# Attention's output projection in float16 planes: one more weight product is scaled into range, and the undoing factor moves into the reciprocal row sums

## What is computed

```python
def _mxfp4_matmul(x, codes, scales, block_size=BLOCK):
    w = codes * jnp.repeat(scales, block_size, axis=0)
    return x @ w
...
q = _mxfp4_matmul(x, wq_codes, wq_scales) + bq
k = _mxfp4_matmul(x, wk_codes, wk_scales) + bk
v = _mxfp4_matmul(x, wv_codes, wv_scales) + bv
...
scores = jnp.einsum('bqhd,bkhd->bhqk', q, k) / jnp.sqrt(jnp.float32(HEAD_DIM))
attn = jax.nn.softmax(scores, axis=-1)
out = jnp.einsum('bhqk,bkhd->bqhd', attn, v).reshape(B, S, NUM_HEADS * HEAD_DIM)
return _mxfp4_matmul(out, wo_codes, wo_scales) + bo
```

## Time and profile before

| | |
|---|---|
| median of 3 runs | 992.88 us (992.58 to 993.28) |
| span of the profiled execution | 991.7 us |
| busy: PE / PEld | 927.3 us (94%) / 585.8 us (59%) |
| busy: DVE / ACT / POOL | 718.4 (72%) / 648.1 (65%) / 641.0 us (65%) |
| chain that ended last | PE 75%, DVE 11%, POOL 4%, issue 4%, DMA 3%, ACT 3% |
| `b_out` matmuls | 3 x 256 from L109 to L111, means 367, 281 and 279 ns |
| `b_v` matmuls, 256 columns, float16 | 3 x 256, mean 273 ns each |

### The profile page before, as it was taken

How to read it: one execution, slowest core, us unless ns; L and a number is a source line. 1 busy time by engine, 2 the same in 40 slices (tenths; PEclk the granted TensorE clock), 3 DMA queues, 4 the chain that set the end, 5 groups by cost and what they waited for, 6 DMA issues and landing times.

```text
span 991.7 us, 18415 instructions
## 1 busy us (share of the span) xinstructions
PE 927.3 (94%) x5772; PEld 585.8 (59%) x5772; DVE 718.4 (72%) x2006; ACT 648.1 (65%) x1410; POOL 641.0 (65%) x599
## 2 busy tenths in 40 slices
PE   4999779999999999999999999999999999988967
PEld 3766456556556556555655655655565557775556
DVE  7863389887777777777778777777876689782327
ACT  5634337787777777776876777777776878433511
POOL 2467759896587668779766676776675655246711
PEclk9999989999999999999999999999999999998979
DMA  9968654687676779868886775677565656545782
GB/s 341 394 204 303 234 191 112 129 160 149 97 150 106 154 145 199 187 140 190 169 168 96 135 154 97 138 143 119 100 124 85 119 103 106 174 151 195 282 349 87
DMA packets 302976, 165.57 MB, mean 167 GB/s; under 512 B 278176, under 2 KB 285600, under 8 KB 300832
## 3 DMA queue, kind: packets, MB, share of 16 engines
q1 hardware_dynamic: 297696, 146.56, 63.8%
q0 software_dynamic: 3072, 9.44, 2.8%
q10 hardware_dynamic: 2112, 8.39, 2.1%
HBM read 68.93 MB, written 28.31 MB: 98 GB/s over the span
## 4 chain that ended last, share of the span: by engine, by line
PE 75%; DVE 11%; POOL 4%; issue 4%; DMA 3%; ACT 3%; DVEq 0%; POOLq 0%; ACTq 0%; SPq 0%
PE b_o L109 5%; PE b_o L110 5%; PE b_o L111 5%; PE b_p L109 5%; PE b_p L111 5%; PE b_p L110 5%; PE b_s L109 5%; PE b_s L110 5%; PE b_s L111 5%; PE b_out L109 3%; PE b_out L110 3%; PE b_out L111 3%; PE b_v L109 3%; PE b_v L111 3%; PE b_v L110 3%
## 5 line engine op out<-in xcount | busy, mean ns | idle before, releaser
L2423 POOL TENSOR_TENSOR h<-pr,h 128x512 f16<-128x512 f32 x256 | 293.7, 1160 | 185.9 <-ACT h L1151 180.3
L1141 ACT ACTIVATE pr<-b_s,nmax,kappa 128x512 f32<-128x512 f32 x256 | 197.7, 775 | 39.0 <-DVE nmax L1880 37.6
L1877 DVE TENSOR_SCALAR_CACHE_REDUCE junk<-b_s 128x512 bf16<-128x512 f32 x256 | 175.2, 684 | 30.6 <-PE b_s L111 29.7
L1151 ACT ACTIVATE h<-pr 128x512 f16<-128x512 f32 x256 | 153.7, 627 | 0.5
L1904 DVE SCALAR_TENSOR_TENSOR x<-b_out,rinv,x 128x256 f32<-128x256 f32 x256 | 110.4, 472 | 45.8 <-PE b_out L111 45.8
L109 PE MATMUL b_p<-xh,w 128*128 128x512 f16 x256 | 98.6, 385 | 2.4 <-DVE xh L1681 2.4
L109 PE MATMUL b_s<-kT,qT 128*128 128x512 f16 x256 | 97.6, 381 | 1.0 <-DVE qT L1823 0.7
L110 PE MATMUL b_p<-xh,w 128*128 128x512 f16 x256 | 98.0, 383 | 0.0
L111 PE MATMUL b_p<-xh,w 128*128 128x512 f16 x256 | 98.0, 383 | 0.0
L109 PE MATMUL b_o<-pT,v 128*128 128x512 f16 x256 | 97.1, 379 | 0.0
L110 PE MATMUL b_o<-pT,v 128*128 128x512 f16 x256 | 97.0, 379 | 0.0
(11 more groups left out here) (212 smaller groups left out, 2276.8 us busy)
## 6 DMA issues: line engine op xcount, KB each, us to landing
raw<-in_experts SPq DMA_DIRECT2D x32, 768.0 KB, 7.4
raw_cs<-in_heads SPq DMA_DIRECT2D x16, 1024.0 KB, 5.6
zrows<-zero ACTq DMA_DIRECT2D x4, 2048.0 KB, 17.5
z<-zrows SPq DMA_DIRECT2D x16, 512.0 KB, 4.0
zrows<-zero SPq DMA_DIRECT2D x16, 512.0 KB, 3.1
zl<-zrows SPq DMA_DIRECT2D x16, 512.0 KB, 10.5
rows<-xn SPq DMA_DIRECT2D x8, 512.0 KB, 10.4
pT<-h SPq DMA_TRANSPOSE x256, 3.3
```

Source lines behind the costliest of these rows:

```text
L1141: act.activation(pr[n % 4][:], b_s[n % 3][:], ACT.Exp, bias=nmax[:, u % 2, i:i + 1], scale=kappa[:, s:s + 1], accum_out=rsum[:, u % 2, i:i ...
L1151: act.activation(h[n % 4][:, 0, :], pr[n % 4][:], ACT.Copy).then_inc(q["p_high"], 1)
L1877: dve.tensor_scalar(junk[n % 2][:], b_s[n % 3][:], 0.0, None, ALU.add, ALU.max, accum_out=peaks[:, n % 2:n % 2 + 1]).then_inc(q["peak_read ...
L2423: pool.tensor_tensor(h[n % 4][:, 1, :], pr[n % 4][:], h[n % 4][:, 0, :], ALU.subtract).then_inc(q["p_split"], 1)
```

## The change

`wo` and `oT` become float16 planes. So that both lie in float16's range, the output weights get a power-of-two factor of their own, as v has. `norms`, `bound`, `halves` and the factors get a second column: `vo_scale` and `vo_undo`. `squares` gets a third square, of the product of the output weights, and now waits for all four products (`w_mul` at 4p + 4) and for `qk_normed`, since it writes into `square_qk`; `squares_qk` waits for `normed`. `scales` works on two columns and computes `o_undo`, the product of both undoing factors and a constant; `oT` is made with a fixed factor 2**-23. In `sums` the reciprocal goes into `rsum_o`, and a TENSOR_SCALAR multiplies it by `o_undo` into `rinv`. The output weights are scaled into range on GpSimd (a fourth `range_weights`), are split behind v's in place of ahead of them, and in `prepare` move from r = 5 to r = 7; `load_qk` moves from r = 6 to behind the transposes of r = 7. In the written-out part of pair 1 the products of v and o stand one behind the other.

```diff
 ZBITS = 23
+OBITS = 23
...
 ones = m.keep("ones", [P, P])
-norms = m.keep("norms", [P, 2])
-bound = m.keep("bound", [P, 1])
-halves = m.keep("halves", [P, 1], I32)
+norms, bound = m.keep("norms", [P, 4]), m.keep("bound", [P, 2])
+halves = m.keep("halves", [P, 2], I32)
...
 peaks = m.keep("peaks", [P, 2])
-v_scale = m.keep("v_scale", [P, 2], I32)
-v_undo = m.keep("v_undo", [P, 2], I32)
+vo_scale, vo_undo = (m.keep(n, [P, 2, 2], I32) for n in ("vo_scale", "vo_undo"))
+o_undo, rsum_o = m.keep("o_undo", [P, 2]), m.keep("rsum_o", [P, 4])
...
 w = [[m.at((A, Bm)[s] + 8192 * k, f"w{k}_{s}", [P, 6, D], F16) for k in range(2)] for s in range(2)]
-wo = [[m.at((A, Bm)[s] + 8192 * k + 3072, f"wo{k}_{s}", [P, 2, D], F32R) for k in range(2)] for s in range(2)]
+wo = [[m.at((A, Bm)[s] + 8192 * k + 3072, f"wo{k}_{s}", [P, 2, D], F16) for k in range(2)] for s in range(2)]
...
 zl = [m.at(o, f"zl{i}", [P, 4 * D]) for i, o in enumerate(z_place)]
-oT = [[m.at(Bm + 16384 + 4096 * s + 2048 * k, f"oT{k}_{s}", [P, S], F32R) for k in range(2)] for s in range(2)]
+oT = [[m.at(Bm + 16384 + 4096 * s + 2048 * k, f"oT{k}_{s}", [P, S], F16) for k in range(2)] for s in range(2)]
...
             pe.wait_ge(q["v_sum"], 2 * B * (p - 1) + 7)
-        pe.matmul((b_v[:, 0:2] if p else b_p0[:, D:D + 2]), ones[:], norms[:], start=True, stop=True).then_inc(q["normed"], 1)
+        pe.matmul((b_v[:, 0:4] if p else b_p0[:, D:D + 4]), ones[:], norms[:], start=True, stop=True).then_inc(q["normed"], 1)
...
         if n % (2 * B) == 0:
-            pe.wait_ge(q["aw_ready"], 4 * pair_of(n) + 4)
+            pe.wait_ge(q["aw_ready"], 4 * pair_of(n) + 3)
...
             if u % (2 * B) == 0:
-                pe.wait_ge(q["aw_ready"], 4 * pair_of(u) + 3)
+                pe.wait_ge(q["aw_ready"], 4 * pair_of(u) + 4)
...
     def outputs(u):
-        p = pair_of(u) % 2
...
             act.wait_ge(q["out_done"], 2 * (u - 1))
-        act.activation(oT[u % 2][0][:], b_o[:], ACT.Copy, scale=v_undo[:, p:p + 1].bitcast(F32)).then_inc(q["o_hi"], 1)
+        act.activation(oT[u % 2][0][:], b_o[:], ACT.Copy, scale=2.0 ** -OBITS).then_inc(q["o_hi"], 1)
...
     def squares_qk(p):
...
             act.wait_ge(q["qk_normed"], p)
+            act.wait_ge(q["normed"], p)
...
     def squares(p):
-        act.wait_ge(q["w_mul"], 4 * p + 3)
+        act.wait_ge(q["w_mul"], 4 * p + 4)
...
                        accum_out=norms[:, 0:1])
-        act.activation(square[:, S:], bvb[p % 2][:], ACT.Square, accum_out=norms[:, 1:2]).then_inc(q["squared"], 1)
+        act.activation(square[:, S:], bvb[p % 2][:], ACT.Square, accum_out=norms[:, 1:2])
+        act.wait_ge(q["qk_normed"], p + 1)
+        act.activation(square_qk[:, 0:S], raw_of(3)[0].rearrange("p t f -> p (t f)"), ACT.Square, accum_out=norms[:, 2:3]
+                       ).then_inc(q["squared"], 1)
...
     def scales(p):
...
         dve.wait_ge(q["normed"], p + 1)
-        own.did(dve.tensor_reduce(bound[:], b_v[:, 0:2] if p else b_p0[:, D:D + 2], X, ALU.add))
+        own.did(dve.tensor_reduce(bound[:], (b_v[:, 0:4] if p else b_p0[:, D:D + 4]).rearrange("p (a b) -> p a b", b=2), X, ALU.add))
...
         own.wait()
-        own.did(dve.tensor_scalar(v_scale[:, s:s + 1], halves[:], -float(2 ** ZBITS), 202.0 * 2 ** ZBITS, ALU.mult, ALU.add))
-        own.did(dve.tensor_scalar(v_undo[:, s:s + 1], halves[:], float(2 ** ZBITS), 51.0 * 2 ** ZBITS, ALU.mult, ALU.add))
+        own.did(dve.tensor_scalar(vo_scale[:, s, :], halves[:], -float(2 ** ZBITS), 202.0 * 2 ** ZBITS, ALU.mult, ALU.add))
+        own.did(dve.tensor_scalar(vo_undo[:, s, :], halves[:], float(2 ** ZBITS), 51.0 * 2 ** ZBITS, ALU.mult, ALU.add))
         own.wait()
-        dve.tensor_scalar(bvb[s][:], bvb[s][:], v_scale[:, s:s + 1].bitcast(F32), 2.0, ALU.mult, ALU.mult
+        own.did(dve.scalar_tensor_tensor(out=o_undo[:, s:s + 1], in0=vo_undo[:, s, 0:1].bitcast(F32), scalar=2.0 ** (OBITS + 1),
+                                         in1=vo_undo[:, s, 1:2].bitcast(F32), op0=ALU.mult, op1=ALU.mult))
+        dve.tensor_scalar(bvb[s][:], bvb[s][:], vo_scale[:, s, 0:1].bitcast(F32), 2.0, ALU.mult, ALU.mult
...
         dve.wait_ge(q["exp_done"], 4 * u + 4)
-        dve.reciprocal(rinv[:, u % 4, :], rsum[:, u % 2, :]).then_inc(q["rinv_ready"], 1)
+        if u > 0:
+            dve.wait_ge(q["rinv_ready"], u)
+        own.did(dve.reciprocal(rsum_o[:], rsum[:, u % 2, :]))
+        own.wait()
+        s = pair_of(u) % 2
+        dve.tensor_scalar(rinv[:, u % 4, :], rsum_o[:], o_undo[:, s:s + 1], None, ALU.mult).then_inc(q["rinv_ready"], 1)
...
     def outputs(u):
-        p = pair_of(u) % 2
         dve.wait_ge(q["o_hi"], u + 1)
-        dve.scalar_tensor_tensor(out=oT[u % 2][1][:], in0=b_o[:], scalar=v_undo[:, p:p + 1].bitcast(F32),
-                                 in1=f32(oT[u % 2][0][:]), op0=ALU.mult, op1=ALU.subtract).then_inc(q["o_lo"], 1)
+        dve.scalar_tensor_tensor(out=oT[u % 2][1][:], in0=b_o[:], scalar=2.0 ** -OBITS, in1=oT[u % 2][0][:],
+                                 op0=ALU.mult, op1=ALU.subtract).then_inc(q["o_lo"], 1)
...
     def fills():
...
         own.did(dve.memset(mhalf[:], -0.5))
+        own.did(dve.memset(norms[:, 3:4], 0.0))
...
     def range_weights(p, j):
-        codes, s = raw_of(j)[0], p % 2
+        codes = raw_of(j)[0]
...
             pool.wait_ge(q["scale_ready"], p + 1)
-            scale = v_scale[:, s:s + 1].bitcast(F32)
+            scale = vo_scale[:, p % 2, j - 2:j - 1].bitcast(F32)
...
     def planes(p, j):
...
     def high_weights(p, j):
-        if j == 3:
-            pool.wait_ge(q["w_mul"], 4 * p + 4)
-        else:
-            pool.wait_ge(q["w_scaled"], 3 * p + j + 1)
+        pool.wait_ge(q["w_scaled"], 4 * p + j + 1)
...
     def low_weights(p, j):
         hi, lo = planes(p, j)
-        pool.wait_ge(q["w_hi"], 4 * p + (1, 2, 4, 3)[j])
-        pool.tensor_tensor(lo, raw_of(j)[0], f32(hi) if j == 3 else hi, ALU.subtract).then_inc(q["aw_ready"], 1)
+        pool.wait_ge(q["w_hi"], 4 * p + j + 1)
+        pool.tensor_tensor(lo, raw_of(j)[0], hi, ALU.subtract).then_inc(q["aw_ready"], 1)
...
             scale_weights(p, 3)
-        elif r == 5:
-            high_weights(p, 3)
-            low_weights(p, 3)
...
             low_weights(p, 2)
+        elif r == 7:
+            range_weights(p, 3)
+            high_weights(p, 3)
+            low_weights(p, 3)
...
     range_weights(0, 2)
+    high_weights(0, 2)
+    low_weights(0, 2)
+    range_weights(0, 3)
     high_weights(0, 3)
-    high_weights(0, 2)
     low_weights(0, 3)
-    low_weights(0, 2)
...
     scale_weights(1, 2)
+    scale_weights(1, 3)
...
     probs_low(5, 3)
-    scale_weights(1, 3)
...
     probs_low(6, 0)
-    high_weights(1, 3)
+    high_weights(1, 2)
...
     probs_low(6, 2)
-    high_weights(1, 2)
-    low_weights(1, 3)
+    low_weights(1, 2)
     probs_low(6, 3)
-    low_weights(1, 2)
+    range_weights(1, 3)
...
     probs_low(7, 1)
+    high_weights(1, 3)
     values(7)
+    low_weights(1, 3)
...
             load_vo(p + 1)
-        if r == 6 and p < PAIRS - 2:
+        if r == 7 and p < PAIRS - 2:
             load_qk(p + 2)
-        if r == 7 and p < PAIRS - 2:
```

## The result

| kernel | median (runs) | ratio to the kernel before, 95% interval |
|---|---|---|
| before, measured beside it | 992.65 us (20) | |
| the changed kernel | 989.51 us (20) | 0.9961 (0.9944 to 0.9977) |
| the same, in a second series | 990.61 us (12), before 992.5 | 0.9991 (0.9969 to 1.0012) |

The first series has the kernel 0.4% faster, the second within 0.2%. Single runs of either kernel scatter over 8 us and more. Against the sum of -1.2 us stand -3.1 and -1.9 us by the medians, and -2.8 and -3.1 by the spans of the profiled executions (991.7 us before, 988.9 and 988.6 after).

What follows compares the result with a forecast made beforehand. TensorE was taken to bound the attention stage, busy 99.27 of 100 us. The terms, -9.0 + 2.8 + 1.8 + 1.2 + 0.6 + 1.0 + 0.4 = -1.2 us, gave a median of 991.7 us, range 987 to 998.5.

Steps and rivals of the forecast that it cites:

- Rival C: Scaling of `bvb` in `scales` blocked by GpSimd, making `values(7)` late by 1.06 us: +6.4 us in six pairs, 998.1; chance 0.12.
- D: Reciprocals' multiplication blocked through two GpSimd subtractions, stopping TensorE 0.4 us in some 35 units: +14, about 1005 us; chance 0.05.
- Rival F: The six `output` matmuls keep their spacing, so only the costs are left: +7.8, 1000.7 us; chance 0.05.
- Term 1: Six 256-column matmuls in each of 128 `output` calls go from float32r to float16: 0.07 us a call, -9.0 us.
- Term 2: Prologue: `squares(0)` waits for all four products and has a third square, delaying `silu(12)` 2.2 us and `axn`: +2.8 us.
- Term 3: Weights of pair 1: TensorE waits 1.0 us at `norm(1)` and 0.8 at `values(7)`: +1.8 us, between 1.0 and 3.0.
- Term 4: Third square in the six later pairs delays the first weight load of `output`: 0.2 us each, +1.2 us.
- Term 5: Reciprocals' multiplication in `sums`, blocked by GpSimd: 0.6 us behind q and k squares, 1.0 in head and tail; bounds 0 and 4.
- Small terms: `values` with r = 3 gives 0.07 us back to a wait, +0.4 us in six pairs; moved weights and `load_qk` free.
- Rival B: Prologue and pair 1 cost 2 us in place of 4.6, chains shrinking when pushed, tail nothing: 988.2 us; chance 0.30.
- A: The forecast itself, all terms as priced: 991.7 us, with its own range of 990 to 994; chance 0.41.
- E: Faster `output` moves `bks` ahead of GpSimd, saving 0.94 us in six pairs: 986.1 us; chance 0.07.

## Why the prediction was right or wrong, point by point

- **What bounds the kernel:** right for the loop. TensorE stays the bound there, and most of the 47 us more of VectorE's time passed under it; outside the loop it did not.
- **The prediction's own signs:** two of those that it names for being wrong came in. The start of attention has not moved to where it should (150.5 and 149.7 us against 150.7), and TensorE has gaps in units that had none: near 210, before the `scores` of unit 7, and in units 56 to 60. "No change that can be told" holds for the second series; in the first the interval ends at 0.9977, a small gain, to which the prediction gave 0.37. (Its chances for slower, C, D and F, add up to 0.22 where it writes 0.21.)
- **Term 1 (-9.0):** right. In the loop 16 calls a pair at 0.07 us; float16 alone took 8.7 us from the stretch between the first `scores` and the last `b_out`. Rival F is refuted. The six matmuls were priced well, but "the `oT` planes ... no difference" was wrong: they got 0.15 us shorter by the constant scale, a part of the diff that I had read as neutral. With the shorter weight loads it took 0.18 us a pair out of the stall behind the squares of q and k. This is 1 us of the 2.2 us by which the loop beat its forecast; the rest is in terms 4 and 5.
- **Term 2 (+2.8):** the step to `silu(12)` was right: 2.2 us, and 2.1 to 2.8 in nine traces. At `axn` 1.1 to 2.6 us arrived, less than 2.8, in part because GpSimd held fewer of VectorE's additions (the last one took 1.39 us at 131.72 before, and 0.43 at 133.49 after). The step that failed is "nothing later gives the time back": at the first `scores` nothing is left in the median, since the first projections take 5.2 us at full clock in six of nine executions, where they took 7.8 before. The prediction has no word on the clock in that stretch, though the kernel before shows 0.50 there, behind the idle time that the same edit moves.
- **Term 3 (+1.8):** right in mechanism, the waits at `norm(1)` and `values(7)` were 1.55 and 0.67 against 1.0 and 0.8. The stage lost 4.65 us against float16 alone, but 2.0 of these belong to the reciprocals; with them left out it loses 2.7, inside the bounds of 1.0 to 3.0. The step that failed is that I stopped at `values(7)`: VectorE was held up by 1.9 us in the chain of scales (`halves` and `o_undo` take 1.10 us each in place of 0.17 and 0.16) and passed 0.63 us of it on to q and k of unit 7. The 1.36 us in the trace of the changed kernel has 0.73 from the reciprocals in it.
- **Term 4 (+1.2):** right in mechanism, wrong in size: six stalls of 0.07 us, 0.4 in all. The template was the stalled group of the old type with its slow loads and slower `oT`; with the range alone in float32r the same group stalls by 0.10.
- **Term 5 (0.6 + 1.0):** the row was right (0.85 us in most of 64, and `outputs` just in time). In the loop it cost nothing, not even 0.6. Outside it cost 4 us, not 1.0, and none of it in units 0 to 4: 2.0 in units 4 to 8, half of that by a wait that I did not see at all, ScalarE's exponentials behind `rinv_ready`, which now comes after the product; 1.0 to 1.3 in units 56 to 60; and 0.8 behind them. I gave the bound of 4 and took a value near its lower end, because the covers that I had measured were those of the loop.
- **Small terms:** the wait at `values` with r = 3 grew by 0.07 us, as forecast. The moved weights and `load_qk` cost nothing.
- **Rival B** is nearest in time (988.2; the median is 989.51), though against the kernel before the second series (-1.9 us) lies nearer to A. Its reason holds in half: the prologue and the weights of pair 1 cost about 1.7 to 2.7 us in place of 4.6, but not because chains shrink when pushed (pair 1 cost more than its price, and the clock paid for the prologue), and the tail cost 1.8 to 2.1 us and not nothing. **Rival C** did not fire, though its margin was real. `bvb` keeps 0.10 us ahead of GpSimd, against 0.23 in the earlier trace rows:

```profile
483.29 0.35 DVE L1864 TENSOR_SCALAR bvb<-bvb,vo_scale 128x256 f32<-128x256 f32 x1
483.39 1.26 POOL L2430 TENSOR_TENSOR h<-pr,h 128x512 f16<-128x512 f32 x1 [3.48 <-ACT h L1151]
```

  In units 4 to 8 that mechanism did fire, at `halves` and `o_undo`. **Rivals D and E** did not: `bks` stays at 1.16 us.

That the total came close is luck: errors of 2 to 4 us with different signs cancelled. The prologue was 3 to 4 us better, the loop 2.2 better, units 0 to 8 were 2.7 to 3.1 worse, and the attention behind the loop 1.5 to 1.7 worse.

## What to carry to other kernels

Cost an edit separately for the steady loop and for each written-out stretch: an operation that is free in 48 units out of 64 cost 4 us in the other 16, in those stretches where no idle time stood behind it. When a semaphore's increment moves behind a new instruction, list everyone who waits for that semaphore; an exponential that only needed the old read waited for the new product. And treat idle time ahead of a stretch at the lower clock as its possible cause: an edit that moves the idle time moves the slow stretch too.

## What the runs showed of the hardware

- A scale that is a constant in place of one value per partition: 594 against 684 ns for a 128x512 ACTIVATE from PSUM, 690 against 750 for VectorE's operation behind it, with the same types.
- A weight load of 128 columns takes 0.10 us in float16 and 0.19 in float32r; behind a wait the second load started 0.02 against 0.11 us after the first. In the stream a matmul of 256 columns starts 0.118 us after the last one in float32r and 0.109 in float16, and a group of six, with the matmul on either side, costs 0.07 us more in float32r.
- The first projections, up to the first `scores`, take 5.2 us at a granted clock of 1.00 and 6.5 to 7.9 us at a mean of 0.65 to 0.79.
- A VectorE operation of one column and two inputs in SBUF (`o_undo`) takes 1.10 us when GpSimd works, 0.16 when not. The Trainium skill (SBUF — State Buffer, Who interferes with whom) says that a VectorE instruction with two SBUF inputs contends with a GpSimd instruction that reads SBUF; these rows agree.
- The multiplication of the reciprocals, 128x4, takes 0.23 us on VectorE at its least and 0.85 in the median, beside GpSimd's subtractions; on GpSimd itself it takes 0.27.
